# A fused two-layer block on one core: output product in pieces, one variance, a row finished in the next attention, experts' weights on another queue

## The reference

```python
x = layernorm(x + L0_attn(x))      # differential attention, 16 heads of size 8, RMS norm of each head
x = layernorm(x + L0_ffn(x))       # gate/up/down, both operands rounded to FP4 in blocks of 16
x = layernorm(x + L1_attn(x))      # rotary, 16 query heads, 4 key heads of size 64, causal here in two halves
x = layernorm(x + L1_ffn(x))       # router: 1 of 8 experts for each token; own layernorm with gain and bias
```

```python
router_logits = xt @ Wr + br
gates = max(softmax(router_logits)); idx = argmax(...)
xn = (xt - mu) * rsqrt(var + 1e-5) * ln_g + ln_b
h = relu(xn @ W1[idx] + b1[idx]);  y = (h @ W2[idx] + b2[idx]) * gates
```

## Time and profile before

| what | value |
|---|---|
| median of 3 runs | 1311.98 us (1310.96 to 1313.03) |
| the profiled execution, its own time | 1311.07 us |
| its span, first to last instruction | 1309.3 us |
| busy: PE / DVE / ACT / POOL | 1027.1 / 784.8 / 642.1 / 424.7 us |
| mean granted PE clock | 0.826 of full speed |

### The profile page before, as it was taken

How to read it: one execution, slowest core, us unless ns; L and a number is a source line. 1 busy time by engine, 2 the same in 40 slices (tenths; PEclk the granted TensorE clock), 3 DMA queues, 4 the chain that set the end, 5 groups by cost and what they waited for, 6 DMA issues and landing times.

```text
span 1309.3 us, 20064 instructions
## 1 busy us (share of the span) xinstructions
PE 1027.1 (78%) x7121; PEld 525.3 (40%) x7121; DVE 784.8 (60%) x1821; ACT 642.1 (49%) x1581; POOL 424.7 (32%) x512
## 2 busy tenths in 40 slices
PE   2698757899989775998998875999989728799744
PEld 1122321233455421554455431454455518345534
DVE  4788348883787395762776476761776351566421
ACT  1177513774475153775367143676266405156313
POOL 3000110301787004001787102201586330387311
PEclk7579955889999855998999665998998958799957
DMA  5300071000030004111012003211000032100051
GB/s 152 89 3 2 31 180 34 2 2 10 1 97 10 1 2 128 51 34 40 8 58 49 1 2 103 75 34 32 9 1 1 1 132 77 39 1 2 1 185 61
DMA packets 54305, 56.83 MB, mean 43 GB/s; under 512 B 13688, under 2 KB 46016, under 8 KB 53440
## 3 DMA queue, kind: packets, MB, share of 16 engines
q1 hardware_dynamic: 53184, 53.47, 14.1%
q0 software_dynamic: 1024, 2.10, 0.5%
HBM read 43.16 MB, written 16.20 MB: 45 GB/s over the span
## 4 chain that ended last, share of the span: by engine, by line
PE 54%; DVE 18%; ACT 9%; issue 8%; DMA 4%; SPq 3%; POOL 3%; POOLq 0%; ACTq 0%; DVEq 0%
PE ps L1539 9%; DVE mx L941 8%; PE ps L1568 7%; PE ps L1522 6%; PE ps L1583 5%; PE ps L1603 4%; PE ps L1613 4%; PE ps L1369 3%; ACT PROB L1227 3%; PE ps L1676 3%; PE ps L1456 2%; PE ps L1363 2%; DMA qst<-mrow 2%; PE ps L1497 2%; PE ps L1554 1%
## 5 line engine op out<-in xcount | busy, mean ns | idle before, releaser
L941 DVE TENSOR_REDUCE mx<-ps 128x1 f32<-128x512 f32 x512 | 323.5, 684 | 97.8 <-PE ps L1497 95.6
L1227 ACT ACTIVATE PROB<-ps 128x512 f32<-128x512 f32 x512 | 276.8, 603 | 179.4 <-PE ps L1522 177.9
L570 POOL TENSOR_SCALAR PROB<-PROB,rsum 128x128 f32<-128x128 f32 (+3 forms) x224 | 229.4, 1036 | 63.0 <-DVE rsum L1072 62.6
L1269 ACT ACTIVATE PROB<-ps,mx 128x128 f32<-128x128 f32 (+3 forms) x256 | 132.9, 525 | 154.5 <-DVE mx L1067 152.2
L1522 PE MATMUL ps<-qst,kst 27*128 27x512 bf16 x512 | 145.3, 452 | 58.7 <-DMA qst<-mrow 40.8
L1497 PE MATMUL ps<-kst,qst 24*128 24x512 bf16 x512 | 158.3, 479 | 39.0 <-DVE mx L941 27.4
L1539 PE MATMUL ps<-PROB,v 128*32 128x256 f32 x2048 | 183.3, 451 | 3.0 <-ACT OREG L1236 2.6
L1067 DVE TENSOR_REDUCE mx<-ps 128x1 f32<-128x128 f32 (+3 forms) x256 | 113.1, 484 | 69.8 <-PE ps L1586 69.7
L551 POOL CAST mparts<-mx 128x16 bf16<-128x16 f32 x32 | 7.0, 217 | 451.3 <-DVE mx L941 405.2
L1603 PE MATMUL ps<-cst,PROB 128*128 128x128 f32 x640 | 113.3, 298 | 30.1 <-ACT PROB L1284 9.8
L1522 PEld LDWEIGHTS ps<-qst,kst 27*128 27x128 bf16 x512 | 33.1, 93 | 192.7 <-ACT PROB L1227 100.8
(11 more groups left out here) (211 smaller groups left out, 1383.6 us busy)
## 6 DMA issues: line engine op xcount, KB each, us to landing
wexp<-expert_rows SPq DMA_DIRECT2D x44, 514.0 KB, 4.9
qk_terms<-RREG SPq DMA_DIRECT2D x48, 128.0 KB, 2.1
kst<-qk_terms SPq DMA_DIRECT2D x16, 192.0 KB
qst<-qk_terms SPq DMA_DIRECT2D x16, 192.0 KB
RREG<-sorted_x SPq DMA_DIRECT2D x4, 704.0 KB, 6.0
sorted_y<-RREG SPq DMA_DIRECT2D x4, 704.0 KB, 3.9
expert_rows<-in_L_ffn_W_dram SPq DMA_DIRECT2D x1, 2048.0 KB
expert_rows<-in_L_ffn_W_dram SPq DMA_DIRECT2D x4, 512.0 KB
```

Source lines behind the costliest of these rows:

```text
L570: pool.tensor_scalar(tile, tile, rsum1[:, 2 * v + half:2 * v + half + 1], None, ALU.mult).then_inc(scaled1, 1)
L941: dve.tensor_reduce(mx0[:, ga % 2, col:col + 1], ps[:, max_bank(k, MAX_SLOT[n]), :], AX, ALU.max, negate=True).then_inc(slot0_free, 1)
L1227: act.activation(prob0[:, s % 2, q % 4, q % 8 // 4], ps[:, s0_banks[q % len(s0_banks)], :], ACT.Exp, scale=float(HD0) ** -0.5).then_inc(ex ...
L1269: act.activation(prob1[:, half, at:at + w], ps[:, a1_bank(v, half), 0:w], ACT.Exp, bias=mx1[:, col:col + 1], accum_out=sum1[:, col:col + 1 ...
```

## The change

Five edits of the order, and one of the arithmetic.

1. The output product is cut into 8 pieces of 4 products and moved into the steps (-1, 0) to (0, 1) of the following overlap, into PSUM bank 6 in place of 5. The last gate/up product, its silu and its multiplication go to (-1, 1).
2. One variance: the experts' own layernorm takes its mean as zero and its variance from the first one (var * inv^2), so the second `centre` and `scale` go; `both_scales`, one more square root and one multiplication with a broadcast come in. Both square roots stand at (1, 1) on ACT.
3. The routing moves later by some 5 to 8 steps, the experts' tiles by 7 (first tile at step 33 in place of 26); the feed-forward's rounding on DVE and POOL moves earlier, and POOL does two rounds of it before the scatter.
4. The bias product moves from (17, 1) to (5, 1), its sum to (5, 2). The rest of the row (gathered rows, `centre`, square root, `scale`) becomes `finish_row` and runs at v = 12, 13, 14 and 15 of the next `attention1`; `yt` gets a buffer of its own, and `attention1` waits for `y_kept` (the last copy of a tile) and, before the first rotary product, for `ys_out` (the store of `ys` landed) in place of `moe_sum`. For the last row `finish_row` comes at the end.
5. The 11 weight transfers of a row leave SP's queue and are issued by ACT, one every third step from (5, 0); SP's read of the sorted rows moves behind the row transfers of group 3; the next row's input is fetched before the output is given out.

```diff
+ROW_PRODUCTS = {(-1, 0): (0, 1), (-1, 1): (2,), (-1, 2): (3, 4), (-1, 3): (5,), (0, 0): (6,), (0, 1): (7,)}
+LAST_GATE_UP = (-1, 1)
-    _at = 25 + 35 * _n // (2 * NTILE)
+    _at = 32 + 32 * _n // (2 * NTILE)
-WEIGHTS_AFTER = {1: (0, 1, 2), 2: (3, 4, 5), 3: (6, 7, 8), 5: (9,), 6: (10,)}
+WEIGHTS_AT = {((20 + 3 * n) // 4, (20 + 3 * n) % 4): n for n in range(NTILE)}
+FINISH_V = (12, 13, 15)
...
 # DVE
+            def both_scales(i):
+                dve.wait_ge(stdC, 3 * i + 1)
+                step(dve.reciprocal(stC[:, 1], stC[:, 0])); settle()
+                step(dve.tensor_tensor(var2, mvC[:, :, 1], stC[:, 1], ALU.mult)); settle()
+                dve.tensor_tensor(var2, var2, stC[:, 1], ALU.mult).then_inc(varC, 1)
...
-                if (s, c) == (0, 3):
-                    centre(XP, bnC, mvC, varC)
-                if (s, c) == (2, 1):
-                    scale(XP, ZC, mvC, stC, stdC, 3 * i + 2, lnC)
+                if (s, c) == (1, 2):
+                    both_scales(i)
+                if (s, c) == (2, 1):
+                    dve.wait_ge(stdC, 3 * i + 2)
+                    step(dve.reciprocal(inv2, stC[:, 0])); settle()
+                    dve.tensor_tensor(ZC[:, :, :], XP[:, :, :], inv2...broadcast_to([P, NT, E]), ALU.mult).then_inc(lnC, 1)
...
+            def finish_row(i, piece):
+                if piece == 0:
+                    dve.wait_ge(bias2_added, i + 1)
+                    dve.wait_ge(yt_in, 16 * NT * (i + 1))
+                    for t in range(NT):
+                        ins = dve.scalar_tensor_tensor(XP[:, t], yt[:, t], gate[:, t:t + 1], XP[:, t], ALU.mult, ALU.add)
...
+                elif piece == 1:
+                    centre(XP, bnC, mvC, varC)
+                else:
+                    scale(XP, XP, mvC, stC, stdC, 3 * i + 3, lnC)
...
 # ACT
+            def fetch_expert(i, j):
+                if j == 0:
+                    act.wait_ge(tiles_ready, i + 1)
+                n = NTILE * i + j
+                if n >= RING:
+                    act.wait_ge(down1, n - RING + 1)
+                e = act.value_load(tile_expert[0:1, j:j + 1], min_val=0, max_val=NE - 1)
+                act.dma_start(wexp[:, n % RING, :], expert_rows[bass.ds(e, 1), :, :]...).then_inc(wexp_in[n % RING], 16)
...
+                if (s, c) == (1, 1):
                     std_c(3 * i + 1)
+                    act.wait_ge(varC, 3 * i + 2)
+                    act.activation(stC[:, 0], var2, ACT.Sqrt, bias=eps[:, 0:1]).then_inc(stdC, 1)
...
 # PE, experts_stream
+                for piece in ROW_PRODUCTS.get((s, c), ()):
+                    if piece == 0:
+                        pe.wait_ge(oT_ready, 8 * (i + 1))
+                    t = piece // 2
+                    for w in range(4 * (piece % 2), 4 * (piece % 2) + 4):
+                        ins = pe.matmul(ps[:, 6, P * t:P * (t + 1)], oT[:, w, P * t:P * (t + 1)], wo1_sb[:, w, :],
+                                        start=(w == 0), stop=(w == 7))
...
 # PE, attention1
                 if r:
-                    pe.wait_ge(moe_sum, r)
+                    pe.wait_ge(y_kept, NTILE * r)
...
 # POOL, overlap: the first two rounds of the hidden layer's rounding stand before the scatter
+                    if hidden and g == 2:
+                        pool.wait_ge(hs_ready, r + 1)
+                        next(rounds)
+                        next(rounds)
                     if 0 <= i and g == 2:
                         scatter_tokens(i)
```

More of the change, by code:

```diff
@@ L467, in overlap @@
                     if 1 <= r:
-                        for j in WEIGHTS_AFTER.get(g, ()):
-                            fetch_expert(r - 1, j)
-                        if g == 1:
+                        if g == 3:
                             fetch_sorted(r - 1)
@@ L505, in _ @@
                     fetch_again(r + 2)
+                if 1 <= r:
+                    give_out(r - 1)
                 if r == -1:
@@ L612, in overlap @@
                         max_parts0(k, g)
+                    if hidden and g == 2:
+                        pool.wait_ge(hs_ready, r + 1)
+                        next(rounds)
+                        next(rounds)
                     if 0 <= i and g == 2:
                         scatter_tokens(i)
-                    if hidden and g in (2, 3):
-                        if g == 2:
-                            pool.wait_ge(hs_ready, r + 1)
-                        next(rounds)
                     if hidden and g == 3:
@@ L870, in experts_stream @@
                     dve.wait_ge(oh_ready, i + 1)
+                if (s, c) == (5, 2):
+                    dve.wait_ge(bias2_ready, i + 1)
+                    dve.tensor_tensor(XP[:, :, :], XP[:, :, :], tiles(RB), ALU.add).then_inc(bias2_added, 1)
                 if (s, c) in SORTED_TURN:
@@ L1113, in attention1 @@
                     turn(k, nx, v)
+                    if r and v in FINISH_V:
+                        finish_row(r - 1, FINISH_V.index(v))
                     if nx < BATCH:
@@ L1124, in _ @@
                 overlap(r + 1)
+            for piece in range(len(FINISH_V)):
+                finish_row(BATCH - 1, piece)
         @block.scalar
@@ L1200, in ffn_stream @@
                     silu(r, SILU[s, c], 6)
+                if r > 0 and (s, c) == LAST_GATE_UP:
+                    silu(r, NT - 1, 0)
                 if (s, c) in HID_KEEP:
@@ L1305, in attention1 @@
                     turn(k, nx, v)
+                    if r and v == FINISH_V[1] + 1:
+                        std_c(3 * r)
                     if k < BATCH and v in GATE_UP_V:
                         silu(k, GATE_UP_V[v], 0)
-                if k < BATCH:
-                    silu(k, GATE_UP_V[V_END], 0)
             turn_next(0)
@@ L1328, in _ @@
                 overlap(r + 1)
+            std_c(3 * BATCH)
         @block.tensor
@@ L1462, in ffn_stream @@
                     gate_up(r, GATE_UP[s, c], 6)
+                if r > 0 and (s, c) == LAST_GATE_UP:
+                    gate_up(r, NT - 1, 0)
                 if (s, c) in HID_TURN:
@@ L1574, in scores1 @@
                     n, g = P * (qt + 1), w // 2
-                    if v == 0 and r:
-                        pe.wait_ge(moe_sum, r)
                     if v % 4 == 0:
@@ L1645, in attention1 @@
                 pe.wait_ge(slot0_free, SLOTS * min(r + 2, BATCH))
+                if r and alone(r - 1):
+                    pe.wait_ge(y_kept, NTILE * r)
                 for i in range(2):
@@ L1672, in attention1 @@
                         gate_up(k, GATE_UP_V[v], 0)
-                pe.wait_ge(oT_ready, 8 * (r + 1))
-                for t in range(NT):
-                    for c in range(8):
-                        ins = pe.matmul(ps[:, 5, P * t:P * (t + 1)], oT[:, c, P * t:P * (t + 1)], wo1_sb[:, c, :],
-                                        start=(c == 0), stop=(c == 7))
-                ins.then_inc(y1_ready, 1)
-                if k < BATCH:
-                    gate_up(k, GATE_UP_V[V_END], 0)
             pe.wait_ge(first_in, 48)
```

121 lines of the change are left out of this document (58 added, 63 removed).

## The result

The changed kernel takes 1278.22 us (median of 4 runs, 1277.80 to 1279.09) against 1312.51 us for the kernel before in the same session (1310.96 to 1315.56): a ratio of 0.9748, 95% interval 0.9711 to 0.9785. The forecast was 1275.0, with a range of 1255 to 1300. The profiled execution took 1277.80 us.

A forecast was written before the change was run, and what follows sets the result against it. The prediction saw a chain of stages, not one saturated engine. Rows 1 and 2 at -14.3 each (-28.6), row 3 -10 and overlap(4) +2 gave -36.6 us: 1274.5, with the median's 0.9 offset 1275, range 1255 to 1300.

The forecast's parts named there:

- hole at step 16: Rows 1 and 2, step (4, 0): PE's wait for row transfers queued behind weights on SP goes, -12.8 us each.
- Issue on ACT: Rows 1 and 2: eleven weight fetches issued by ACT cost +3 us each, between 0 and 11.2.
- Output product in pieces: Start of overlaps 1 and 2: cutting the product gains 8 us each, between 3.4 and 11.
- one variance: Rows 1 and 2, (1, 1): ACT's second square root waits some 2.5 us for DVE; +2 us, bounds -1 and +4.
- Finish in the attention: Rows 1 and 2, v = 12 to 15: deferred DVE work and square root mostly show, +3.5 us of at most 6.6.
- Row 3: Into attention1(3): entry -14, finish +2.5, ACT's issue +1.5, transfers beside the scatter +1, shorter routing chain -1; sum -10 us.
- The last stretch: Overlap(4): scaling off the scatter's way -1, weights beside scatter and sorted rows +1.5, ACT's issue +1.5; sum +2 us.
- ACT half open: Rival, chance 0.17: six to eight of eleven fetches hold the chain, 22 us in place of 9; 1288 us.
- slower: Rival, chance 0.08: the issue on ACT alone makes the kernel slower, up to 1337 us if fully open.
- row transfers stay late: Rival, chance 0.05: row transfers stay late behind weights of the other queue, 25.7 us come back; 1300 us.
- The start gives little: Rival, chance 0.10: lower clock in the pieces, gain 3.4 in place of 8, and an ACT stall of 4; 1288 us.
- Everything hides: Rival, chance 0.12: start gains 11, issue 0, steps -4, each row 10 us better; 1255 us.

The follow-up runs named there:

- the order alone: Kernel before, weight fetches still on SP's queue but one row group later, sorted rows' read likewise, so group 2's row transfer precedes the routing wait: 1294.26 us, ratio 0.9862.
- the run with one block: Changed kernel with all eight pieces of the output product issued together at step (-1, 0): 1286.93 us, ratio 0.9832.
- the other two edits: Changed kernel with two variances again and the values' products ahead of the row's own work; with POOL's passes behind the scatter as well: 1263.97 us, ratio 0.9651.
- the run with the weights on SP: Changed kernel with its eleven weight fetches given back to SP's queue, behind the row transfers of groups 2 to 7: 1280.57 us, ratio 0.978.

## Why the prediction held, and where it was off

The time was 3 us above the forecast, and part of that closeness is luck. Rows 1 and 2 fell short of their sums by 4.2 and 4.9 us, and row 3 and the last stretch beat theirs by 2.7 and 3.6; inside the rows, too, errors of several microseconds cancel. Rows 1 and 2, with the parts taken from the starts of the score products:

```
us                                              forecast   row 1   row 2
hole at step 16                                   -12.8    -13.2   -12.5
product to step 16, hole left out (-8, +2)         -6       -0.3    -1.7
steps 16 to 63 (issue +3, steps moved 0)           +3       +2.2    +2.8
step 63 to the first query/key product             -2       -0.8    -0.8
attention, with the finish                         +3.5     +2.0    +2.7
sum                                               -14.3    -10.1    -9.4
```

*The hole*: its disappearance was forecast to 0.4 us, and its worth was not: 7.3 and 6.6 us by the order alone. The prediction took the steps behind the hole as if they kept their speed; six of them lost the higher clock, and from step 16 to 63 5.8 and 5.6 us came back, most of it by the clock. (DVE and POOL did run a little at the start of the hole, 0.35 and 1.37 us of 498 to 510; the prediction has nothing running.)

*Issue on ACT, +3*: 0, within the noise. The +2.2 and +2.8 between steps 16 and 63 match the term's size by chance. Against the run with the order alone (103.7 us in either row) the changed kernel needs 100.1 and 100.9 there: everything else in the change, the moved steps above all, gained 3.7 and 2.9, inside that term's bounds of -4 and +5, and the removed hole took 5.8 and 5.6. The pace among the tiles, 66.5 us for 30 steps or 2.22 each, is as forecast (2.2 to 2.3).

*Output product in pieces, -8, and one variance, +2*: this is the step that failed, both terms by size. The shorter start is there (17.9 to 10.0 us, 17.7 to 8.5), but 7.7 and 7.6 us are lost again by step 16. The one variance was taken to keep ACT waiting some 2.5 us for DVE; it waited 3.91 between the roots. Computing the second variance again returns 3.3 and 3.4 us by step 16, so the one variance cost that as it was placed, near its bound of +4; placed a step earlier it cost 2.3 and 2.4 less. The pieces were worth 4.2 and 3.9 us by step 16 in the run with one block, half of the 8. That is near the bound of 3.4 that the prediction gave for the lower clock in the pieces, but its reason did not come: the clock was 0.84 over the first 10 us behind the product's start in row 1 and 1.00 over the first 8.5 in row 2, much as the choice of the upper half assumed. The prediction also took POOL's passes ahead of the scatter for free: they cost 1.6 us between steps 0 and 16 when they alone are moved back, and 3.3 in row 1 when the other two edits are in.

*Finish in the attention, +3.5*: 2.0 and 2.7 from the first query/key product to the next output product, a little less than the term. At v = 14 two table loads of 1.28 and a root of 0.30 hold ACT from 669.29 to 672.18, and PE takes up again at 673.95 after 1.02 us of waiting for ACT.

```profile
669.29 1.28 ACT L1169 ACT_TABLE_LOAD   x1
670.59 0.30 ACT L1169 ACTIVATE stC<-mvC,eps 128x4 f32<-128x4 f32 x1
670.90 1.28 ACT L1304 ACT_TABLE_LOAD   x1
```

The pair costs 2.9 us, with no drain between load and root, as in the earlier trace rows; by the Trainium skill (ScalarE: Activation LUTs, What ACT_TABLE_LOAD costs) two switches would be an estimated 5.3, and the rows decide.

*Row 3, -10*: -12.7. The entry to the attention, timeline of ACT and PE:

```profile
1089.61 0.27 ACT L1210 COPY RREG<-ps 128x128 f32<-128x128 f32 x1 [0.79 <-PE ps L1405]
```

```profile
1090.02 1.96 PE L1694 MATMUL ps<-wv_sb,xT 128*128 128x256 f32 x8 [0.45 <-ACT RREG L1210]
1091.82 1.88 PE L1613 MATMUL ps<-xT,wk_sb 128*128 128x512 f32 x4
```

The first query/key product starts 2.2 us behind the last copy (forecast: within 3). From the last down product it is 2.5 us in place of 12.3, and from there to the next output product 2.0 more than before. The -14 for this entry came out where the prediction looked, at the second rotary pair (5.6 us behind the end of the last copy for 20.0), but 2.7 of it are lost at the next pair, which the prediction did not look at: DVE waits 3.35 us for POOL, which issues the four gathers (1094.02 to 1098.83) ahead of its rotary sum.

```profile
1100.22 2.73 DVE L1078 SCALAR_TENSOR_TENSOR RREG<-ps,bqk,rope_sb 128x512 f32<-128x512 f32 x4 [3.35 <-POOL MREG L571]
```

Product to first tile became 2.3 us longer: the shorter routing chain did not show, since POOL's passes held DVE's comparisons for 1.1 and 2.6 us. The term that the sum lacked is the tiles themselves, 25.8 us in place of 33.0, at a clock of 1.00 in place of 0.85:

```profile
1080.20:1113.20 33.00, 29.52 (x216) 28.44 (x216) 3.69 (x17) 18.82 (x65) 0.00 (x0) 0.85 0.21 75
```

```profile
1063.50:1089.30 25.80, 22.92 (x200) 22.27 (x198) 3.41 (x16) 17.60 (x61) 0.00 (x0) 1.00 0.45 144
```

They also hold fewer matmul groups of other work (200 for 216). Without this -7.2 row 3 would have fallen 4.5 us short of its -10.

*The last stretch, +2*: -1.6; its ACT issue of +1.5 is nothing here either. The run with the order alone has 77.5 us there too, for 79.3, so that the -1.6 need not be the change's; no run tells it from chance.

Of the rivals, "ACT half open" and "slower" are refuted by the run with the weights on SP, and "row transfers stay late" by the waits of the changed kernel. "The start gives little" comes near to what rows 1 and 2 did, which miss the forecast by 4.2 and 4.9 us where it has 6.6: its ACT stall of 4 us is there (3.91), its lower clock in the pieces is not. "Everything hides" falls with the give-backs. The forecast thought of the clock for the pieces, and not for the hole.

## What to carry to other kernels

When a small urgent transfer sits behind a wait in one engine's queue, try the order of that queue first: here it did all that a second queue did. Price a removed hole at what the next stage does with the time, at the clock granted there, and not at its length. An operation saved is worth nothing where its engine idles, and costs where the saving makes one engine wait for another: either bring the other's part forward (here one step, 8 us) or put the wait where the waiting engine has nothing else, even if that means doing the work twice (here as much). And time won ahead of a stretch at the lower clock has to be read behind that stretch.

## What the runs showed of the hardware

DVE's TENSOR_TENSOR on two operands in SBUF, 128x32, takes 0.19 us alone and 1.30 and 2.80 us beside POOL's pass over 128x1408; each ends 0.04 us after POOL's pass does (1036.95 and 1036.91, 1040.24 and 1040.20 us), while a reduction with one operand takes 0.19 in the middle of the pass. The Trainium skill (SBUF — State Buffer, SBUF: two separate sides) describes this: a pair of SBUF ports that DVE, with two SBUF inputs, and POOL hold in turn for whole instructions. I had not looked for it in the change, though it moves POOL's passes beside the routing; the trace agrees, and the price was 3.7 us in row 3.

The granted clock came back at step 20 in the kernel with the hole and near step 26 with only the order changed, and at the same time, 519.9 and 519.8 us, in both. Three microseconds on either side, all engines:

```profile
517.00:520.00 3.00, 3.00 (x28) 0.70 (x20) 1.52 (x3) 1.09 (x2) 2.76 (x5) 0.52 0.05 21
520.00:523.00 3.00, 2.77 (x26) 1.08 (x22) 2.74 (x5) 2.47 (x5) 2.92 (x2) 1.00 0.00 0
```

```profile
517.00:520.00 3.00, 3.00 (x27) 0.94 (x19) 2.54 (x5) 1.70 (x4) 0.00 (x0) 0.53 0.61 186
520.00:523.00 3.00, 2.79 (x30) 1.56 (x27) 2.52 (x5) 2.17 (x4) 0.00 (x0) 1.00 0.89 267
```

PE is busy without a break in the three microseconds ahead of the rise in both, at different steps. The 13 us in which PE did nothing moved the rise neither forward nor back; with the hole, PE only had six steps fewer behind it when the rise came, and did those six at the higher clock. Over all fourteen profiles and both rows the clock rose, to stay up for 40 us or more, 68 to 79 us behind the first output product, although the work done by then differs. Why it rises there stays open; no run here varied it alone.
